# Four layers of cross-attention on one core: the joints between stages reordered, and a launch that waits for fewer constants

## The chip, the cores and the metric

One core of one Trainium2 chip runs the whole program in one launch. The metric is the device time of the execution in microseconds (us), lower is better. TensorE (PE) multiplies, VectorE (DVE) and ScalarE (ACT) work element by element, GpSimd (POOL) helps with copies and sums, and SyncE (SP) issues most transfers.

## The reference, cut to what matters

Four layers follow one another on `x` (4 batches of 256 tokens, width 256) with a context of 1601 rows of width 128. What is computed:

```
L0: qn = layernorm(x); q = qn @ Wq / 8;  k, v = ctx @ Wkv         (16 heads of 64)
    x += tanh(gate) * (softmax(q k^T, masked) v) @ Wo
    x += tanh(gate2) * gelu(layernorm(x) @ W1) @ W2
L1: m = ctx_rows @ W_mem; c = softmax(x m^T / 16) m
    x = rmsnorm(x + sigmoid([x, c] @ W_gate + b) * c) * w
L2: mixed = where(expert, rms(x) @ v_qkv, rms(x) @ l_qkv), rotary, causal self-attention
    x += where(expert, ctx @ v_dense, ctx @ l_dense)
    x += cross-attention(rms(x), ctx; 16 heads of 8) @ cdense
    x += where(expert, silu-MLP with v weights, silu-MLP with l weights)
L3: as L1, with its own weights
```

## The kernel before, in words

The program is written engine by engine: each engine has one list of instructions, in the order in which the Python code issues them, and the engines meet only at semaphores (`Signal` objects; `at(turn, n)` is the value to wait for). No scheduler moves anything. All four batches are unrolled one after another (`body(b, ...)`); the stages of a batch form one chain, and only at its end is the next batch's preparation mixed in.

**The launch.** SP issues the first batch's inputs, then the constants through `const()` (L392 to L395), which all count on one semaphore `const_in`. `const_r` (37 matrices of 128x128, 2.3 MB) lands in `const_r_raw`, placed over the tiles `k_hi_lo0` and `k_hi_rows0`; DVE casts it to `const_r` in `const_cast` (L1470). `const_trig` makes a one-hot matrix of the positions, PE multiplies it with the trigonometric tables (`x<-pos_onehot,const_trig`), and `const_tables` (L1488) copies the result to `cos_t` and `sin_t`. POOL's `prologue` (L511) fills the mask rows of the keys and queries of both buffer sets (`fill_keys`, `fill_queries`). Then come the first projections (`prep_q`, `prep_k`), the first value tiles (`first_values`, seven of them), eight partial maxima (`first_max`, reduced by DVE as `max_parts`) and the first pair of heads.

**Pairs.** The sixteen heads of L0 run as eight pairs (`pair(p)`). Within a pair PE makes 13 score tiles (`st`), ACT takes the exponent (`probs`), POOL adds the tiles up (`prob_sums`, the softmax denominators), PE multiplies with the values (`pv`). The projections of the next pair, the value tiles of the next duo (`v_tile`, written to the bank MI) and the maxima of the next pair are spread between them. `sums(i)` (on PE) multiplies `prob_sums` with ones, DVE takes the reciprocal (`recip_sum`) and scales `attn_t` (`normalise`, which then signals `norm`).

**The joints** are the places where one stage ends and the next starts:

- *Output projection*: after pair 7, `sums` for pair 7, then `x<-w_o,attn_t` for pairs 0 to 6 and last for pair 7; DVE adds to `x_b`, computes mean and variance, POOL raises to the power -1/2 (`rstd_work`), DVE writes `x_normed`, PE transposes it. Ahead of three transposes twelve matmuls (`st<-const_r`, the table `WARM`) run whose result nobody reads. POOL clears `v_cross` (L567) right after its power.
- *Cross-attention of L2*: `cross_queries(0)`, `cross_queries(1)`, then 31 maxima before the first scores; at its end `ctx_heads_t` is divided by its sums (`over_sums`, groups 0 to 2 and then group 3) and multiplied with `w_cd`.
- *Down projection of the MLP*: six `hid` steps on DVE, then `pv<-w_down,...`, for each half of the tokens first six tiles of `h_v`, then six of `h_l`; between the halves PE transposes the next batch's `x_normed`.
- *Pair 0 of each batch*: its value tiles stand behind the score steps k0 = 2, 4, 6, 8, and the first of them waits for DVE's `q_lo_shift` of the next pair.

Of the kernel before, what the change touches and what calls it, by code (L numbers as in the profile page):

```python
# [15 lines left out]
F32 = mybir.dt.float32  # L16
F32R = mybir.dt.float32r
I32 = mybir.dt.int32
# [5 lines left out]
P = 128  # L24
# [12 lines left out]
VS = 4  # L37
# [8 lines left out]
CONSTS = 6  # L46
# [93 lines left out]
def program(nc, io):  # L140

    with ExitStack() as ctx:
# [72 lines left out]
        tids = place("type_ids", [P, NT], I32, [a[0]])  # L215
        side(0, "v", [P, KT, 2 * P], F32)
# [9 lines left out]
        craw_const = place("const_r_raw", [P, N_R, P], F32, [base])  # L226
        posi = place("positions_int", [P, NT], I32, [base + 20480])
        posf = place("positions", [P, NT], F32, [base + 21504])
        onehot = place("pos_onehot", [P, 2, NT], F32, [base + 22528])
        ctrig = place("const_trig", [P, N_C - N_CR, P], F32, [base + 24576])  # L230
# [76 lines left out]
        krows_ready = sig("krows_ready")  # L307
# [36 lines left out]
        cc_read, cc_sum, cc_ready, cd_mm = sig("cc_read", primed=True), sig("cc_sum", 2), sig("cc_ready"), sig("cd_mm")  # L344
# [45 lines left out]
        def _(sp):  # L390
# [87 lines left out]
        def _(pool):  # L478
# [33 lines left out]
            def prologue(b, first):  # L512
# [14 lines left out]
                fill_queries(0)  # L527
                fill_queries(1).then_inc(krows_ready.handle, 1)
                queries(b * PAIRS, 0)
                keys(b * PAIRS, 0, 0)  # L530
                keys(b * PAIRS, 0, 1)

            prologue(0, True)

            def body(b, more):
# [29 lines left out]
                pool.wait_ge(wo_mm.handle, wo_mm.at(b))  # L565
# [33 lines left out]
        def _(act):  # L599
# [33 lines left out]

            act.wait_ge(const_in.handle, CONSTS * 16)
            act.activation(tgate[:], gates[:], ACT.Tanh).then_inc(const_r.handle, 1)
            context(0)
            queries(0, 0)
            act.wait_ge(const_t.handle, const_t.at(0))
            keys(0, 0, 0)
            keys(0, 0, 1)  # L640
# [4 lines left out]
            def body(b, more):  # L645
                def pair(p):
# [12 lines left out]
                    for k0 in range(0, KT, 2):  # L659
# [7 lines left out]
                        if v_tile(p, k0):  # L667
                            if p == 0 and k0 == 2:
# [169 lines left out]
        def _(pe):  # L838
# [18 lines left out]
            def prep_q(i, s, b=None):  # L857

                pe.wait_ge(w_split.handle, w_split.at(i))
# [1151 lines left out]
```

## Time and profile before

| | |
|---|---|
| median of 3 runs | 2308.95 us (2303.93 to 2312.57) |
| the profiled execution | 2304.52 us, of which the span of the trace is 2302.7 us |
| PE busy | 2004.1 us (87%) |
| DVE / ACT / POOL busy | 1298.0 / 923.0 / 766.9 us |
| mean granted TensorE clock | 0.921 |

The profile is of one execution. A busy share says how long an engine had an instruction in flight; the chain of waits says which engine each stretch of the run hung on. The granted clock is 1.00 for 2.4 GHz and 0.50 for 1.2 GHz. A matmul of float32 operands can stand as two records in the trace (16 matmuls of the output projection are 32 records).

### The profile page before, as it was taken

How to read it: one execution, taken by the hardware profiler on the slowest of the kernel's cores; microseconds unless marked ns; L12 is line 12 of the kernel's file. 1: busy time of each engine (PE TensorE's matmuls, PEld its weight loads, DVE VectorE, ACT ScalarE, POOL GpSimd, SP SyncE). 2: the span in 40 equal slices, each digit the busy share in tenths (PEclk: the TensorE clock that was granted, in tenths of full speed). 3: DMA queues.
4: the chain of work that ended last, by engine and by line, in shares of the span. 5: the costliest groups of instructions: out<-in, count | busy, mean ns of one | idle time of the engine just before them, and what ended most of it. 6: DMA issues, size and time to landing. Idle time of an engine off the chain costs nothing.

```text
span 2302.7 us, 30843 instructions
## 1 busy us (share of the span) xinstructions
PE 2004.1 (87%) x11940; PEld 1485.0 (64%) x11940; DVE 1298.0 (56%) x2045; ACT 923.0 (40%) x1718; POOL 766.9 (33%) x676
## 2 busy tenths in 40 slices
PE   3999888898899978899889988889888998888986
PEld 2676667556677657655676766765577765775655
DVE  5666335664676623675576753367457664346733
ACT  1455232371355413257045541326415553231731
POOL 3678410000378731000237881100025886100000
PEclk9999999799899999879999998988999999887998
DMA  4000200201000020100100001020010001102000
GB/s 177 9 11 5 112 1 1 83 1 43 29 12 8 12 104 1 42 41 1 48 26 14 8 37 76 1 83 1 23 36 20 10 8 69 44 1 82 1 1 5
DMA packets 18145, 74.16 MB, mean 32 GB/s; under 512 B 2896, under 2 KB 10320, under 8 KB 14544
## 3 DMA queue, kind: packets, MB, share of 16 engines
q1 hardware_dynamic: 17424, 69.56, 8.2%
q10 hardware_dynamic: 576, 2.62, 0.3%
q8 instruction: 96, 1.57, 0.3%
q14 instruction: 49, 0.40, 0.1%
HBM read 71.13 MB, written 1.05 MB: 31 GB/s over the span
## 4 chain that ended last, share of the span: by engine, by line
PE 68%; DVE 17%; ACT 7%; issue 5%; POOL 2%; DMA 1%; SPq 0%; ACTq 0%; POOLq 0%; DVEq 0%
PE x L841 27%; PE pv L841 18%; PE st L841 15%; PE mi L841 6%; DVE k_hi_lo L1459 3%; ACT k_hi_lo L612 2%; DVE max_parts L1540 2%; POOL prob_sums L555 1%; ACT probs L657 1%; DVE q_lo_shift L1549 1%; DVE prob_sums L1847 1%; PE x L965 1%; DVE x_normed L1640 1%; DVE w_pair_lo L1459 1%; ACT ck_stack L745 1%
## 5 line engine op out<-in xcount | busy, mean ns | idle before, releaser
L555 POOL TENSOR_TENSOR prob_sums<-prob_sums,probs 128x512 f32<-128x512 f32 x352 | 453.6, 1289 | 65.0 <-ACT probs L657 19.0
L657 ACT ACTIVATE probs<-st 128x512 f32<-128x512 f32 x416 | 228.5, 596 | 294.4 <-PE st L841 290.8
L1540 DVE TENSOR_REDUCE max_parts<-x 128x1 f32<-128x832 f32 x256 | 250.7, 1020 | 128.6 <-PE x L841 127.4
L539 POOL TENSOR_TENSOR rstd_work<-rstd_work 128x2 f32<-128x2 f32 x24 | 16.7, 695 | 796.4 <-DVE rstd_work L1456 796.4
L1876 DVE TENSOR_REDUCE max_cross<-x 128x1 f32<-128x512 f32 x384 | 238.8, 684 | 72.0 <-PE x L841 70.5
L841 PE MATMUL st<-q_hi_hi,k_hi_lo 128*128 128x256 f32 x832 | 231.2, 309 | 17.6 <-DVE q_lo_shift L1549 17.6
L841 PE MATMUL pv<-probs,v 128*64 128x256 f32 x1664 | 231.6, 397 | 3.7 <-DVE recip_sum L1664 3.7
L841 PEld LDWEIGHTS st<-q_hi_hi,k_hi_lo 128*128 128x128 f32 x832 | 159.9, 192 | 95.5 <-issue 86.2
L841 PE MATMUL st<-q_lo_shift,k_hi_rows 128*128 128x256 f32 x832 | 210.8, 285 | 0.0
L841 PE MATMUL x<-ck_stack,cq_blocks 128*128 128x512 f32 (+1 forms) x512 | 196.4, 458 | 0.1
L841 PEld LDWEIGHTS st<-q_lo_shift,k_hi_rows 128*128 128x128 f32 x832 | 160.7, 193 | 0.1
L1459 DVE TENSOR_TENSOR k_hi_lo<-x,k_hi_lo 64x832 fp32r<-64x832 f32 x128 | 131.0, 1023 | 40.6 <-ACT k_hi_lo L612 39.3
L841 PEld LDWEIGHTS pv<-probs,v 128*64 128x64 f32 x1664 | 101.1, 137 | 81.5 <-issue 27.1
L841 PE MATMUL x<-k_hi_rows,q_hi 128*128 128x416 f32 x512 | 128.9, 361 | 20.3 <-DVE k_hi_lo L1459 17.6
L841 PEld LDWEIGHTS x<-ck_stack,cq_blocks 128*128 128x128 f32 x512 | 107.6, 226 | 43.8 <-DVE max_cross L1876 32.2
L841 PE MATMUL st<-cq_blocks,ck_stack 128*128 128x512 f32 x280 | 121.6, 443 | 10.6 <-ACT cq_blocks L801 6.5
L1664 DVE RECIPROCAL recip_sum<-pv 128x256 f32<-128x256 f32 x32 | 56.2, 1757 | 108.8 <-PE pv L841 108.8
L612 ACT ACTIVATE k_hi_lo<-x 64x832 fp32r<-64x832 f32 x128 | 110.0, 859 | 17.6 <-PE x L841 15.9
L493 POOL TENSOR_SCALAR k_hi_rows<-k_hi_lo 64x1664 fp32r<-64x1664 f32 x64 | 101.0, 1579 | 38.6 <-ACT k_hi_lo L612 35.7
L841 PEld LDWEIGHTS x<-k_hi_rows,q_hi 128*128 128x128 f32 x512 | 85.3, 190 | 32.9 <-issue 28.9
L819 ACT ACTIVATE probs<-st 128x512 f32<-128x512 f32 x140 | 80.3, 604 | 28.4 <-PE st L841 27.9
L841 PEld LDWEIGHTS st<-cq_blocks,ck_stack 128*128 128x128 f32 x280 | 53.7, 194 | 56.5 <-ACT probs_cross L819 17.1
(291 smaller groups left out, 4158.0 us busy)
## 6 DMA issues: line engine op xcount, KB each, us to landing
w_gate_up<-in_wgu SPq DMA_DIRECT2D x4, 3072.0 KB, 10.1
w_ff<-in_w SPq DMA_DIRECT2D x8, 1024.0 KB, 5.7
w_qk<-in_wqk SPq DMA_DIRECT2D x4, 2048.0 KB, 9.0
w_pair<-in_w SPq DMA_DIRECT2D x32, 192.0 KB, 2.3
w_down<-in_wdn SPq DMA_DIRECT2D x4, 1536.0 KB, 13.4
w_dense<-in_wd SPq DMA_DIRECT2D x4, 1024.0 KB, 12.2
mask_ints<-in_mask SPq DMA_DIRECT2D x4, 832.0 KB, 4.3
ctx_t_raw<-in_ctxT SPq DMA_DIRECT2D x4, 832.0 KB, 5.3
```

Source lines behind the costliest of these rows:

```text
L493: pool.tensor_scalar(t["kh1"][0:64, :, c], r32(t["kst"][0:64, :, c]), 1.0, 0.0, ALU.mult, ALU.add)\
L555: pool.tensor_tensor(acc[:, 0], acc[:, 0], prob[:, kt % 4], ALU.add).then_inc(add_pool.handle, 1)
L612: act.activation(par[s]["kst"][0:64, h, j * HALF:(j + 1) * HALF].rearrange("p (c n) -> p c n", c=2), X[j][64 * h:64 * h + 64, :].rearrange ...
L657: act.activation(prob[:, kt % 4], ST[kt % 2][:], ACT.Exp, scale=HD0 ** -0.5).then_inc(p_exp.handle, 1)
L745: act.activation(ks2[gr][:, j * HALF:j * HALF + n], X[j][:, 0:n], ACT.Identity, bias=ck[:, K_OH_CROSS:K_OH_CROSS + 1])\
L819: act.activation(slot(n), st_bank(n), ACT.Exp, scale=float(HC2) ** -0.5).then_inc(pc_exp.handle, 1)
L841: return pe.matmul(out, lhsT, rhs, start=start, stop=stop, skip_group_check=True)
L965: last = pe.transpose(X[0][:, o:o + P], src[:, t, ch * P:(ch + 1) * P], ident)
L1459: return dve.tensor_tensor(out, x, y, op)
L1540: dve.tensor_reduce(mxs[:, qt, h, half:half + 1], X[n % 2][:].rearrange("p (c n) -> p c n", c=2)[:, :, 0:QUART], AX.XY, ALU.max).then_inc( ...
L1664: dve.reciprocal(rec[:], PV[:, NT:2 * NT]).then_inc(recip.handle, 1)
L1876: t = dve.tensor_reduce(mxc[:, qt, h, c:c + 1], bank, AX.X, ALU.max)
```

## The change

What it does, by joint:

1. **Launch.** `const_r` comes in two pieces, into the tile `probs` and into a place behind `k_hi_rows1`; the positions come first. DVE's `const_cast` and `const_trig` move behind the first splits, PE's `pos_onehot` matmuls behind the first two value tiles and into the bank PV, the other value tiles between the maxima. POOL no longer waits for the constants: it fills buffer set 0, does the first pair's copies, and fills set 1 after them. A new semaphore `side_rows` tells PE that set 1 is filled. ACT's `keys` no longer wait for constants.
2. **Last sums.** `sums` of pair 7 stands behind the first seven `w_o` matmuls.
3. **Cross fill.** POOL's clearing of `v_cross` waits until DVE has written `x_normed`.
4. **Pair 0.** The value tiles move from k0 = 2, 4, 6, 8 to 4, 6, 8, 10.
5. **Cross queries.** `cross_queries(1)` stands behind the first four maxima.
6. **Dense (`w_cd`) in parts.** Groups 0 to 2 after the first division, group 3 after the second; each half of the tokens gets its own bank.
7. **Down in parts.** The tile index is the outer loop; PE starts after the fifth `hid` and waits for the sixth ahead of tile 5.

```diff
@@ launch @@
-            const(craw_const[:], io["const_r"])
+            const(posi[:], io["pos"].partition_broadcast(P))
             const(ctrig[:], io["const_f"][:, N_CR:N_C])
             const(wck[:], io["wckv"])
+            const(prob[:].rearrange("p k (c n) -> p (k c) n", n=P), io["const_r"][:, 0:16])
+            const(craw_const[:], io["const_r"][:, 16:N_R])
             const(gates[:], io["gates"].partition_broadcast(P))
             const(rows[:], io["rows"].partition_broadcast(P))
-            const(posi[:], io["pos"].partition_broadcast(P))
...
                 if first:
-                    pool.wait_ge(const_t.handle, const_t.at(0))
-                    pool.wait_ge(x0t_read.handle, x0t_read.at(0))
                     fill_keys(0)
-                    fill_keys(1)
+                    fill_queries(0).then_inc(krows_ready.handle, 1)
...
                 queries(b * PAIRS, 0)
                 keys(b * PAIRS, 0, 0)
                 keys(b * PAIRS, 0, 1)
+                if first:
+                    fill_keys(1)
+                    fill_queries(1).then_inc(side_rows.handle, 1)
+                    pool.wait_ge(side_rows.handle, side_rows.at(0))
...
             for n in range(8):
                 first_max(0, n)
+                if n < VT - 2:
+                    first_values(0, n + 2)
@@ cross fill @@
                 rsqrt(1)
-                pool.wait_ge(wo_mm.handle, wo_mm.at(b))
+                pool.wait_ge(x_in.handle, x_in.at(b, 1))
@@ last sums @@
-                sums(i0 + PAIRS - 1)
...
                     for t in range(TT):
                         for p in ((PAIRS - 1,) if last else range(PAIRS - 1)):
                             m = mm(X[0][:, t * 512:t * 512 + D], attn[:, p, t * P:(t + 1) * P], wo[:, p], p == 0, p == PAIRS - 1)
+                        if not last and t == 0:
+                            sums(i0 + PAIRS - 1)
@@ pair 0 @@
+            if p == 0:
+                return (1, k0 // 2 - 2) if 4 <= k0 < 4 + 2 * VS else None
@@ cross queries @@
                 cross_queries(0)
-                cross_queries(1)
                 for g in range(CPARTS + LEAD):
+                    if g == 4:
+                        cross_queries(1)
                     cross_max(g)
@@ dense (w_cd) in parts @@
-                pe.wait_ge(cc_ready.handle, cc_ready.at(b))
-                for t in range(TT):
-                    for k in range(4):
-                        m = mm(X[0][:, t * D:(t + 1) * D], cx[:, k, t * P:(t + 1) * P], wcd[:, k], k == 0, k == 3)
+                for last in range(2):
+                    pe.wait_ge(cc_ready.handle, cc_ready.at(b, last + 1))
+                    for t in range(TT):
+                        for k in ((3,) if last else range(3)):
+                            m = mm(X[0][:, t * 512:t * 512 + D], cx[:, k, t * P:(t + 1) * P], wcd[:, k], k == 0, k == 3)
@@ down in parts @@
-                pe.wait_ge(hid.handle, hid.at(b * 6 + 5))
+                pe.wait_ge(hid.handle, hid.at(b * 6 + 4))
                 for t in range(TT):
                     n = 0
-                    for e2, x in enumerate((hv, hl)):
-                        for k in range(6):
+                    for k in range(6):
+                        if t == 0 and k == 5:
+                            pe.wait_ge(hid.handle, hid.at(b * 6 + 5))
+                        for e2, x in enumerate((hv, hl)):
```

PE at the output projection (`x<-w_o,attn_t` are its matmuls, `pv<-prob_sums,const_f` is `sums`), before and with the change:

```order
L841 MATMUL pv<-probs,v_1_88 64x256 x6
L841 MATMUL pv<-prob_sums,const_f 64x256 x2
L841 MATMUL x<-w_o,attn_t 128x256 x16
L841 MATMUL st<-const_r 128x512 x12
L965 MATMUL x<-const_f,x_normed 128x128 x4
```

```order
L846 MATMUL pv<-probs,v_1_88 64x256 x6
L846 MATMUL x<-w_o,attn_t 128x256 x7
L846 MATMUL pv<-prob_sums,const_f 64x256 x2
L846 MATMUL x<-w_o,attn_t 128x256 x9
L846 MATMUL st<-const_r 128x512 x12
```

Seven of the sixteen projection matmuls now stand ahead of `sums`, and so ahead of its wait for POOL.

DVE in the launch, from the variance on (`const_r` is the cast of the constants, `pos_onehot` the positions), before:

```order
L1456 TENSOR_SCALAR rstd_work<-mean_var 128x2
L1473 CAST const_r<-const_r_raw 128x4736
L1578 TENSOR_SCALAR x_normed<-x_in,mean_var,rstd_work 128x256 x2
L1477 CAST positions<-positions_int 128x256
L1478 TENSOR_SCALAR expert_mask<-positions 128x256
L1459 TENSOR_TENSOR positions<-positions,expert_mask 128x256
L1456 TENSOR_SCALAR positions<-positions 128x256
L1456 TENSOR_SCALAR pos_onehot<-positions,const_cols 128x256 x2
```

and with the change:

```order
L1470 TENSOR_SCALAR rstd_work<-mean_var 128x2
L1591 TENSOR_SCALAR x_normed<-x_in,mean_var,rstd_work 128x256 x2
L1470 TENSOR_SCALAR xn_t<-st,lnq_scaled 128x256 x2
L1600 CAST xn_t_hi<-xn_t 128x512
L1473 TENSOR_TENSOR xn_t_lo<-xn_t,xn_t_hi 128x512
L1520 CAST w_pair_hi_106<-w_pair 128x384
L1473 TENSOR_TENSOR w_pair_lo_108<-w_pair,w_pair_hi_106 128x384
L1473 TENSOR_TENSOR ctx_t_lo<-ctx_t_raw,ctx_t_hi 128x832 x2
L1531 CAST w_duo_hi<-w_duo 128x256
L1473 TENSOR_TENSOR w_duo_lo<-w_duo,w_duo_hi 128x256
L1487 CAST const_r<-probs 128x2048
L1488 CAST const_r<-const_r_raw 128x2688
```

The cast, and its wait for the constants, now stands behind nine other steps of DVE.

## Rows read from the trace of the kernel before

**Rows 1.** The page: span, busy time, and the chain that ended last.
```profile
span 2302.7 us, 30843 instructions
PE 2004.1 (87%) x11940; PEld 1485.0 (64%) x11940; DVE 1298.0 (56%) x2045; ACT 923.0 (40%) x1718; POOL 766.9 (33%) x676
PE 68%; DVE 17%; ACT 7%; issue 5%; POOL 2%; DMA 1%; SPq 0%; ACTq 0%; POOLq 0%; DVEq 0%
```

**Rows 2.** Launch, in order of time: start us, us, engine, operation, idle before it.
```profile
20.20 0.69 POOL L515 TENSOR_TENSOR rstd_work<-rstd_work 128x2 f32<-128x2 f32 x1 [19.76 <-DVE rstd_work L1456]
26.23 2.63 DVE L1473 CAST const_r<-const_r_raw 128x4736 fp32r<-128x4736 f32 x1 [6.11 <-DMA positions_int<-in_pos]
35.06 0.42 DVE L1491 COPY cos_t<-x 128x256 f32<-128x256 f32 x1 [0.56 <-PE x L841]
36.09 8.94 POOL L501 TENSOR_SCALAR k_hi_rows<-mask_row,const_cols 64x1664 fp32r<-64x1664 f32 x4 [15.20 <-DVE sin_t L1492]
47.58 4.15 DVE L1459 TENSOR_TENSOR k_hi_lo<-x,k_hi_lo 64x832 fp32r<-64x832 f32 x4
53.75 7.54 DVE L1540 TENSOR_REDUCE max_parts<-x 128x1 f32<-128x832 f32 x8 [2.02 <-PE x L841]
63.03 0.55 PE L841 MATMUL st<-q_hi_hi,k_hi_lo 128*128 128x256 f32 x1 [0.97 <-DVE q_lo_shift L1549]
```

**Rows 3.** By tile, over the whole run: shortest/median/longest ns of one, first and last start.
```profile
L1640 DVE TENSOR_SCALAR x_normed<-x_b,mean_var,rstd_work x8: 632/1923/3215, 271.1 to 1957.1; 128x256 f32<-128x256 f32 x8
L1638 DVE TENSOR_SCALAR x_normed<-x_b,rstd_work x16: 346/351/355, 335.5 to 2221.5; 128x256 f32<-128x256 f32 x16
L1516 DVE CAST w_duo_hi<-w_duo x16: 285/530/1676, 39.9 to 1848.8; 128x256 fp32r<-128x256 f32 x16
```

**Rows 4.** PE at the output projection of batch 0, in order of time.
```profile
258.72 0.65 PE L841 MATMUL pv<-prob_sums,const_f 128*64 128x256 f32 x4 [3.41 <-POOL prob_sums L555]
259.31 8.86 PE L841 MATMUL x<-w_o,attn_t 128*128 128x256 f32 x32
274.88 1.11 PE L965 MATMUL x<-const_f,x_normed 128*128 128x128 f32 x4 [3.95 <-DVE x_normed L1640]
277.08 8.74 PE L841 MATMUL x<-h_t,w_ff 128*128 128x256 f32 x32 [1.09 <-DVE h_t L1456]
285.66 7.07 PE L841 MATMUL pv<-w_ff,gelu_t 128*128 128x256 f32 x32
```

**Rows 5.** DVE and POOL there.
```profile
261.21 0.43 DVE L1459 TENSOR_TENSOR attn_t<-attn_t,recip_sum 128x256 f32<-128x256 f32 x1
271.08 3.60 POOL L567 MEMSET v_cross<- 128x3536 f32 x2
```

**Rows 6.** By stretch, batch 0: us, PE busy (records), granted clock, DMA share, GB/s.
```profile
261.00:263.00 2.00, 2.00 (x6) 0.50 0.00 0
286.00:293.00 7.00, 6.73 (x32) 1.00 0.01 2
530.00:532.00 2.00, 2.00 (x6) 0.50 0.00 0
541.00:544.00 3.00, 2.88 (x7) 0.50 0.00 0
```

**Rows 7.** End of the cross-attention of batch 0.
```profile
528.59 5.41 PE L841 MATMUL x<-w_cd,ctx_heads_t 128*128 128x256 f32 x16 [2.31 <-DVE ctx_heads_t L1459]
```

**Rows 8.** The other joints of batches 0 and 1, PE.
```profile
566.61 2.86 PE L841 MATMUL pv<-w_down,h_v 128*128 128x256 f32 x12 [1.85 <-DVE h_l L1459]
421.35 0.58 PE L841 MATMUL mi<-cq_hi,const_r 128*128 128x256 f32 x1 [2.05 <-ACT cq_blocks L794]
633.70 0.35 PE L841 MATMUL mi<-w_duo_hi,ctx_t_hi 128*128 128x256 f32 x1 [2.85 <-DVE q_lo_shift L1459]
```

**Rows 9.** DVE beside the down projection of batch 0.
```profile
568.57 2.01 DVE L1578 TENSOR_SCALAR x_normed<-x_in,mean_var,rstd_work 128x256 f32<-128x256 f32 x2 [0.87 <-POOL rstd_work L515]
577.71 0.69 DVE L1459 TENSOR_TENSOR x_a<-pv,x_b 128x512 f32<-128x512 f32 x1 [0.21 <-PE pv L841]
```

More of the change, by code:

```diff
@@ L45 @@
 EPS = (1e-5, 1e-5, 1e-6, 1e-6, 1e-6, 1e-6, 1e-6)
-CONSTS = 6
+CONSTS = 7
 LNQ_G, LNQ_B, LNF_G, LNF_B, W_IN, W_CROSS, W_POST = range(0, 14, 2)
@@ L215, in program @@
         tids = place("type_ids", [P, NT], I32, [a[0]])
+        craw_const = place("const_r_raw", [P, N_R - 16, P], F32, [a[0] + 1024])
         side(0, "v", [P, KT, 2 * P], F32)
@@ L225, in program @@
         attn = place("attn_t", [P, PAIRS, NT], F32, a)
[L226 to L230, printed above, removed]
+        posi = place("positions_int", [P, NT], I32, [base + 27648])
+        posf = place("positions", [P, NT], F32, [base + 28672])
+        onehot = place("pos_onehot", [P, 2, NT], F32, [base + 29696])
+        ctrig = place("const_trig", [P, N_C - N_CR, P], F32, [base + 31744])
         wck = place("w_ckv", [P, 2, P], F32, [base + 26624])
@@ L526, in prologue @@
                     fill_keys(0)
-                fill_queries(0)
-                fill_queries(1).then_inc(krows_ready.handle, 1)
+                    fill_queries(0)
+                    fill_queries(1).then_inc(krows_ready.handle, 1)
                 queries(b * PAIRS, 0)
@@ L632, in first_values @@
                 values(b, 0, c, ST[c % 2])
+            context(0)
+            queries(0, 0)
+            keys(0, 0, 0)
+            keys(0, 0, 1)
             act.wait_ge(const_in.handle, CONSTS * 16)
             act.activation(tgate[:], gates[:], ACT.Tanh).then_inc(const_r.handle, 1)
[L636 to L640, printed above, removed]
+            act.wait_ge(const_t.handle, const_t.at(0, 1))
             act.wait_ge(types_read.handle, types_read.at(0))
@@ L667, in pair @@
                         if v_tile(p, k0):
-                            if p == 0 and k0 == 2:
+                            if p == 0 and k0 == 4:
                                 act.wait_ge(done.handle, done.at(b, 0))
@@ L859, in prep_q @@
                 pe.wait_ge(w_split.handle, w_split.at(i))
+                if i == 1:
+                    pe.wait_ge(side_rows.handle, side_rows.at(0))
                 if b is not None:
@@ L935, in _ @@
             x0_transposed(0)
+            for n in range(4):
+                mm(PV[:], ident, cc[:].rearrange("p k n -> p (k n)"))
+            prep_q(0, 0, 0)
+            prep_k(0, 0, 0, 0)
+            prep_k(0, 0, 1, 0)
+            for c in range(2):
+                first_values(0, c)
             pe.wait_ge(const_in.handle, CONSTS * 16)
@@ L939, in _ @@
                 for ch in range(2):
-                    last = mm(X[1][:, k * NT:(k + 1) * NT], ctrig[:, tab - N_CR + ch], onehot[:, ch], ch == 0, ch == 1)
+                    last = mm(PV[:, k * NT:(k + 1) * NT], ctrig[:, tab - N_CR + ch], onehot[:, ch], ch == 0, ch == 1)
             last.then_inc(const_r.handle, 1)
-            for n in range(4):
-                mm(PV[:], ident, cc[:].rearrange("p k n -> p (k n)"))
-            prep_q(0, 0, 0)
-            pe.wait_ge(const_t.handle, const_t.at(0))
-            prep_k(0, 0, 0, 0)
-            prep_k(0, 0, 1, 0)
-            for c in range(VT):
-                first_values(0, c)
             for n in range(8):
                 first_max(0, n)
+                if n < VT - 2:
+                    first_values(0, n + 2)
             first_shifts(0)
+            pe.wait_ge(const_t.handle, const_t.at(0))
             def body(b, more):
@@ L1031, in pair @@
                     if p < PAIRS - 1:
-                        if v_tile(p, 2):
-                            d, c = v_tile(p, 2)
-                            pe.wait_ge(v_read.handle, v_read.at(b * DUOS + d, VS if c == 0 else VT))
+                        if v_tile(p, 4):
+                            d, c = v_tile(p, 4)
+                            pe.wait_ge(v_read.handle, v_read.at(b * DUOS + d, VS if c < VS else VT))
                         pe.wait_ge(q_lo.handle, q_lo.at(i + 1))
@@ L1472, in const_cast @@
                 dve.wait_ge(const_in.handle, CONSTS * 16)
-                dve.tensor_copy(cr[:], craw_const[:]).then_inc(const_t.handle, 1)
+                dve.tensor_copy(cr[:, 0:16].rearrange("p k n -> p (k n)"), prob[:].rearrange("p k n -> p (k n)"))
+                dve.tensor_copy(cr[:, 16:N_R], craw_const[:]).then_inc(const_t.handle, 1)
             def const_trig():
@@ L1609, in _ @@
             x0_normed(0)
-            const_trig()
             x0_scaled(0)
-            const_tables()
             split(0, 0)
@@ L1616, in _ @@
             split_v(0, 0)
+            const_cast()
+            const_trig()
             split(0, 1)
@@ L1625, in _ @@
             neg_max(0)
+            const_tables()
             shifts(0, 0)
```

16 lines of the change are left out of this document (7 added, 9 removed).

## Prediction

> **What bounds the kernel now.** I read the page first: PE is busy 87% of the span of 2302.7 us, and the chain that ended last runs on PE for 68% and on DVE for 17% [rows 1]. So the run is one chain of stages, mostly on PE, and a gap in PE at a joint is time of the run, not time hidden behind something else. The second view is PE's waits at the joints in order of time: PE stands 3.41 us for POOL's last addition, 3.95 us for `x_normed` [rows 4], 2.31 us for a division [rows 7], 1.85 us for the last `hid`, 2.05 us for `cross_queries`, 2.85 us for `q_lo_shift` [rows 8]. All of these but the last recur once per batch. The third view is the launch: DVE has its variance at 20.9 us and then stands until 26.23 us for the last constant, and the first scores start at 63.03 us [rows 2]. The fourth is the granted clock by stretch. Behind the long gaps it is at 0.50, the 1.2 GHz level, although PE is busy then; 261 to 263 us follows the 3.41 us gap [rows 6]. So a gap costs twice: its own length, and slow matmuls behind it. The 32 records of the output projection take 8.86 us and the 32 of the first feed-forward product 8.74, against 7.07 for 32 equal ones that run at the full clock [rows 4]: 1.8 and 1.7 us from the clock. One record at full clock is 7.07/32 = 0.22 us.
>
> The sum below is made against the profiled execution, 2304.5 us. That is 4.4 us under the median of the three runs.
>
> **Part by part.**
>
> *Last sums, 4 batches.* PE is free 3.41 us before 258.72, at 255.3 [rows 4]. With the change 14 records (7 matmuls) run at once, 14 x 0.22 = 3.1 us, to 258.4; POOL's sum is there at 258.7 as before; `sums` 0.65 us, to 259.4; 14 records, to 262.5; the last pair's scaled `attn_t` is ready at 261.64, as DVE starts its reciprocal when it did [rows 5]; four records, to 263.4. Before, the projection ended at 268.17. Gain 4.8 us per batch, 19 in all. If the slow clock behind the gap stayed, it would be 3.0 us, the gap that is filled (12 in all): the lower bound.
>
> *Cross fill, 4 batches.* DVE's `x_normed` at this joint takes 632 to 3215 ns a piece, against 351 for the same shape elsewhere [rows 3], and POOL's clearing starts in the same instant, 271.08 us, and lasts 3.60 us [rows 5]. DVE waits for the end of POOL's instruction. With the change POOL starts after it, beside a stretch in which DVE reads PSUM only and then idles; the cleared tile is first written to by `cross_v`, two stages later. The two pieces last 3.77 us in batch 0 and would take 0.7: 3.1 us. The gap of PE ahead of its transposes falls from 3.95 to about 0.9, so some of the 1.7 us of slow feed-forward goes too. I take half, as another gap of 1.09 us follows: 4.0 per batch, 16 in all, between 12 and 19. The Trainium skill (SBUF — State Buffer, section on the two separate sides) describes this: VectorE in a two-port mode and GpSimd share a port pair as an exclusive lock for a whole instruction. The 3215 ns beside the clearing agree.
>
> *Dense (`w_cd`) in parts, 4 batches.* Groups 0 to 2 were divided long before; PE has waited 2.31 us, since 526.3, when it goes on at 528.59 for group 3 [rows 7]. Now 12 of the 16 records fill this wait, 2.6 us, to 528.9; then four, 0.9 us: 529.8. Before, the end was at 528.59 + 5.41 = 534.0. Gain 4.2 us, 17 in all, of which 1.9 per batch is the slow clock (16 records in 5.41 against 3.5 us). Without the clock, 2.3 per batch (9).
>
> *Down in parts.* PE starts 1.85 us earlier [rows 8]; ten of the twelve products per half do not need the sixth `hid`. In batches 0 to 2 the transposes between the halves need the next batch's `x_normed`, ready at 570.6 [rows 9]; the first half (24 records, 5.2 us) now ends at 570.0 instead of 571.8, so PE waits 0.6 us there, and DVE, whose list of small steps left only 0.21 us of slack before `x_a` [rows 9], moves ahead with the transposes. Gain 1.2 us three times and 1.85 in the last batch: 5.
>
> *Cross queries, 4 batches.* The first maximum no longer stands behind the second query block: two records, 0.6 us. The 2.05 us of waiting stay, since they are ACT's time for the first block [rows 8]. DVE's reductions set the pace afterwards, so 0.6 x 4 = 2.4.
>
> *Pair 0.* In batches 1 to 3 PE waited 2.85 us for `q_lo_shift` ahead of the first value tile [rows 8]. The wait moves behind two more score tiles and two `pv` tiles, but the next thing, a maximum, needs DVE's four `k_hi_lo` pieces (4.15 us in the launch [rows 2]), which end where they did. So one wait takes the place of the other; I keep 0.8 us three times: 2.4, between 0 and 6. In batch 0 nothing.
>
> *Launch, once.* DVE sets the pace, and its work up to the last `k_hi_lo` is the same list in another order. Before, it ran from the cast at 26.23 to 47.58 + 4.15 = 51.73 us with one wait of 0.56 (for the tables) [rows 2]: 24.9 us of work, of which 0.8 (the copies of the tables) now stands behind the maxima. With the change it starts at the end of POOL's power, 20.20 + 0.69 = 20.9, and has one new wait, for PE's transposes of `x_normed`, 1.2 us (the length that the transposes have elsewhere [rows 4]): 20.9 + 24.9 - 0.8 + 1.2 = 46.2. The eight maxima follow without the 2.02 us wait (the value tiles ran ahead of them on PE and now run between them): 7.5, to 53.7. From the last maximum to the first scores it took 63.03 - 61.29 = 1.7, and 0.3 of the copies stick out: 55.8 instead of 63.03. The constants are there at 26.2 to 27, before DVE comes to them. Gain 7.
>
> What could eat it: POOL's fills now start at 20.9, beside `x_normed` and the splits; before, they met DVE from 36.09 on. `w_duo_hi` took 1676 ns there and 285 at its shortest [rows 3], so a collision costs DVE about 1.4 us. As many collisions as before are in the 24.9 us already. Three more, and a slow PE behind its wait for the positions, which must pass before the maxima, would leave 1 us; none at all would give 12. Where DVE reads PSUM it isn't held: four `k_hi_lo` take 4.15 us beside POOL's fills [rows 2]. I take 7.
>
> By the skill's rule of the lock (same page and section; it also covers two-input operations against a GpSimd operation that reads SBUF) every step of DVE in 21 to 42 us that reads SBUF twice could lose a fill's whole length. By the trace it is about 1.4 us for a step that meets a fill, and that is what the sum contains.
>
> *Sum*: 19 + 16 + 17 + 5 + 2.4 + 2.4 + 7 = 69 us. 2304.5 - 69 = 2235.5. As the runs' median lies 4.4 us above the profiled one, I say 2237.
>
> **The rivals.**
>
> *The slow clock stays.* The gaps shrink but PE's clock falls behind them as before, since small waits remain at each joint (0.3 to 1.1 us). For it: behind the joint into the MLP, whose gaps no part of the change touches, the clock is at 0.50 as well [rows 6]. Against it: it is full in the second feed-forward product, which has no gap ahead of it [rows 6]. Then the joints give 12 + 12 + 9 + 5 + 2.4 + 2.4 and the launch 7: 50 us, 2255. Chance 0.22.
>
> *The launch gives nothing*, because POOL's fills and DVE's splits now collide from the start: 69 - 6 = 63 us, 2242, or 2246 with a lost microsecond at each batch's first pair. It differs from the forecast mostly in place. Chance 0.15.
>
> *Better than the sum*: the clock effects in full and the launch with few collisions, 69 + 3 + 5 + 4 = 81 us, 2224. Chance 0.12.
>
> *Slower.* PE would be held to a lower clock because it idles less. The chain has 68% of the span on PE, 1566 us [rows 1]; each per cent of clock lost there costs 15.7 us, so a mean granted clock of 0.921 that fell by more than 4.4%, below 0.88, would eat all 69 us. At a fall of 5% the time is 2235.5 + 78 = 2314. Against it: the clock reads 1.00 where PE is densest and 0.50 behind gaps [rows 6]. The Trainium skill (TensorE: Matmul & The Clock Gate, Part 1) says the same: the half rate is the resting state and activity lifts it; its power limit concerns several busy cores. Chance 0.02, and 0.02 for a result within 0.5%. That the change doesn't do what it says is excluded for the orders of instructions, which are written out.
>
> **How the numbers follow.** Forecast 0.47 (2230 to 2243), slow clock 0.22, launch 0.15, better 0.12, same 0.02, slower 0.02. The likeliest time is 2237. The range reaches to the better case and to the slow clock with 4 us of run-to-run difference: 2218 to 2258. 0.5% of this kernel is 11.5 us, about what a measurement can tell from no change; every case but the last two is faster by more.
>
> **What would show it.** In the changed profile: no wait of PE for `prob_sums` over 0.5 us and `w_o` done about 8 us after the last `pv`; `x_normed` at this joint under 0.4 us a piece; `w_cd` without its 2.31 us wait; the granted clock at 1.00 behind these joints; first scores at 56 us; mean clock above 0.93. The slow clock rival is right if `w_o` and the first feed-forward product still need over 8.5 us. The forecast is wrong if a stage of equal work (pairs 1 to 7, the cross-attention between its joints) becomes longer than before.

## The result and the profile after

| | before | with the change |
|---|---|---|
| median of 4 runs on one chip | 2307.18 us (2303.93 to 2312.57) | 2244.31 us (2240.4 to 2249.35) |
| ratio, 95% interval | | 0.9729 [0.9711, 0.9748] |
| profiled execution / span | 2304.52 / 2302.7 us | 2243.16 / 2241.4 us |
| mean granted TensorE clock | 0.921 | 0.935 |

The change takes 61.3 us off the span; 69 were predicted. The median lies 7 us above the predicted 2237 and inside the range of 2218 to 2258. The page of the changed kernel, as [rows 1] of before:

```profile
span 2241.4 us, 30844 instructions
PE 1978.9 (88%) x11940; PEld 1467.1 (65%) x11940; DVE 1287.9 (57%) x2046; ACT 923.3 (41%) x1718; POOL 765.9 (34%) x676
PE 68%; DVE 19%; ACT 7%; issue 4%; POOL 2%; ACTq 0%; POOLq 0%; DVEq 0%
```

PE does the same 11940 matmuls in 25 us less, which is mostly the clock; the other 36 us were idle time. The chain is still 68% PE. The line numbers have moved: the matmul helper is L846 now (L841 before), the transposes L974 (L965).

**The joints one by one.** I cut both traces into stages at the same instructions (the first score, DVE's write of `x_b`, the first `w_ff` matmul and so on) and compared the lengths. Each number is the difference of two starts; minus is faster:

| stage | batch 0 | 1 | 2 | 3 | gain | predicted |
|---|---|---|---|---|---|---|
| start to first scores | -2.96 | | | | 3.0 | 7 |
| first scores to the first `attn_t` (pair 0) | +0.44 | +0.99 | +0.90 | +0.94 | -3.3 | 2.4 |
| last `attn_t` to `x_b` (last sums) | -4.69 | -4.63 | -4.78 | -4.67 | 18.8 | 19 |
| `x_b` to `x<-h_t,w_ff` (cross fill) | -3.50 | -3.03 | -3.04 | -3.49 | 13.1 | 16 with the next row |
| feed-forward | +0.12 | +0.26 | -1.41 | +0.17 | 0.9 | |
| up to the first cross maximum (cross queries) | -0.48 | -0.89 | -0.43 | -2.03 | 3.8 | 2.4 |
| cross-attention and `w_cd` (dense) | -4.14 | -4.88 | -4.19 | -3.17 | 16.4 | 17 |
| MLP to `x_a` (down) | -2.26 | -1.03 | -2.27 | -1.21 | 6.8 | 5 with the next row |
| `x_a` to the next first scores | +0.09 | +0.91 | +2.08 | | -3.1 | |

These rows give 56.4 us. The other 5 lie in stages that the change doesn't touch; 3.75 of them in one place, the self-attention of batch 3, where the granted clock before was 0.55 (2054 to 2063 us) and is now 1.00. So the orders of matmuls did most of what the sum says. Two rows are off, the launch and pair 0, and a smaller one is the feed-forward behind the cross fill. The last row, `x_a` to the next first scores, is not the change's alone: it is 46.5, 44.5 and 44.5 us before, and in kernels that leave the down projection as it was it also lies anywhere between 44.4 and 46.6.

**The output projection**, PE and then DVE and POOL, in order of time, as [rows 4, 5]:

```profile
252.19 3.29 PE L846 MATMUL x<-w_o,attn_t 128*128 128x256 f32 x14
255.69 0.65 PE L846 MATMUL pv<-prob_sums,const_f 128*64 128x256 f32 x4 [0.20 <-POOL prob_sums L560]
256.27 4.15 PE L846 MATMUL x<-w_o,attn_t 128*128 128x256 f32 x18
260.07 3.11 PE L846 MATMUL st<-const_r 128*128 128x512 f32 x12
264.10 0.66 PE L974 MATMUL x<-const_f,x_normed 128*128 128x128 f32 x4 [0.92 <-DVE x_normed L1654]
265.84 8.86 PE L846 MATMUL x<-h_t,w_ff 128*128 128x256 f32 x32 [1.09 <-DVE h_t L1470]
```

```profile
263.31 0.73 DVE L1654 TENSOR_SCALAR x_normed<-x_b,mean_var,rstd_work 128x256 f32<-128x256 f32 x2 [0.82 <-POOL rstd_work L544]
264.17 3.57 POOL L572 MEMSET v_cross<- 128x3536 f32 x2 [0.89 <-DVE x_normed L1654]
```

The wait for `prob_sums` is 0.20 us instead of 3.41. All 32 projection records (14 + 18) run near 0.23 us each: the slow stretch behind the old gap is gone. The two pieces of `x_normed` take 0.73 us together, with the clearing behind them, and PE waits 0.92 us instead of 3.95. But the first feed-forward product still takes 8.86 us against 7.07 at the full clock. That is the part of the cross fill that didn't come.

**The two other joints**, as [rows 7, 8]:

```profile
514.96 3.62 PE L846 MATMUL x<-w_cd,ctx_heads_t 128*128 128x256 f32 x16
...
554.14 0.66 PE L859 MATMUL st<-const_f,x_normed 128*128 128x128 f32 x4 [0.69 <-DVE x_normed L1591]
```

`w_cd` runs in one piece without a wait, 3.62 us instead of 2.31 of waiting and 5.41 of work. In the down projection the predicted new wait of 0.6 us, for the next batch's `x_normed`, is there with 0.69.

**Pair 0 of batch 1.** Where before had one wait of 2.85 us [rows 8], there are three:

```profile
616.10 0.36 PE L846 MATMUL mi<-w_duo_hi,ctx_t_hi 128*128 128x256 f32 x1 [0.69 <-DVE q_lo_shift L1473]
...
618.19 0.61 PE L846 MATMUL x<-k_hi_rows,q_hi 128*128 128x416 f32 x2 [1.15 <-DVE k_hi_lo L1473]
620.27 0.62 PE L846 MATMUL x<-k_hi_rows,q_hi 128*128 128x416 f32 x2 [1.47 <-DVE k_hi_lo L1473]
```

0.69 + 1.15 + 1.47 = 3.31 us. The maxima now meet DVE's four `k_hi_lo` pieces with too little in front of them. Before, the value tiles behind them covered those pieces.

**The launch.** DVE, then POOL, then PE, as [rows 2]:

```profile
34.07 1.62 DVE L1493 TENSOR_SCALAR expert_mask<-positions 128x256 f32<-128x256 f32 x1
35.72 1.74 DVE L1473 TENSOR_TENSOR positions<-positions,expert_mask 128x256 f32<-128x256 f32 x1
37.50 1.64 DVE L1470 TENSOR_SCALAR positions<-positions 128x256 f32<-128x256 f32 x1
39.17 1.89 DVE L1470 TENSOR_SCALAR pos_onehot<-positions,const_cols 128x256 f32<-128x256 f32 x2
...
45.73 4.15 DVE L1473 TENSOR_TENSOR k_hi_lo<-x,k_hi_lo 64x832 fp32r<-64x832 f32 x4
```

```profile
33.97 3.23 POOL L496 TENSOR_SCALAR k_hi_rows<-k_hi_lo 64x1664 fp32r<-64x1664 f32 x2
37.29 3.36 POOL L504 TENSOR_SCALAR k_hi_rows<-mask_row,const_cols 64x1664 fp32r<-64x1664 f32 x2
```

```profile
41.21 3.47 PE L846 MATMUL pv<-pos_onehot,const_trig 128*128 128x256 f32 x8 [7.56 <-DVE pos_onehot L1470]
...
60.07 0.55 PE L846 MATMUL st<-q_hi_hi,k_hi_lo 128*128 128x256 f32 x1 [0.97 <-DVE q_lo_shift L1564]
```

Three small steps of DVE on the positions take 1.6 to 1.7 us each, and the two of `pos_onehot` 1.89 together. 1.6 to 1.7 us is the length of one of POOL's instructions beside them (3.23/2 and 3.36/2). The first scores start at 60.07 us, not at 56.

### The profile page after: what moved, and what is told of

Its sections match the earlier page's. It is cut to its first block, busy times and chain, and to the rows that moved or that the text cites. A ratio compares the mean times of both kernels' runs of the same rounds, so it can differ in the third digit from the quotient of the medians.

```text
span 2241.4 us, 30844 instructions
## 1 busy us (share of the span) xinstructions
PE 1978.9 (88%) x11940; PEld 1467.1 (65%) x11940; DVE 1287.9 (57%) x2046; ACT 923.3 (41%) x1718; POOL 765.9 (34%) x676
## 4 chain that ended last, share of the span: by engine, by line
PE 68%; DVE 19%; ACT 7%; issue 4%; POOL 2%; ACTq 0%; POOLq 0%; DVEq 0%
PE x L846 26%; PE pv L846 18%; PE st L846 16%; PE mi L846 6%; DVE k_hi_lo L1473 3%; ACT k_hi_lo L617 2%; DVE max_parts L1555 1%; DVE max_cross L1890 1%; ACT probs L662 1%; POOL prob_sums L560 1%; DVE q_lo_shift L1564 1%; DVE prob_sums L1861 1%; PE x L974 1%; ACT ck_stack L750 1%; DVE recip_sum L1768 1%
## 5 line engine op out<-in xcount | busy, mean ns | idle before, releaser
L846 PE MATMUL st<-q_hi_hi,k_hi_lo 128*128 128x256 f32 x832 | 230.9, 309 | 17.8 <-DVE q_lo_shift L1564 17.8
L846 PE MATMUL pv<-probs,v 128*64 128x256 f32 x1664 | 231.2, 397 | 3.7 <-DVE recip_sum L1678 3.7
L846 PEld LDWEIGHTS st<-q_hi_hi,k_hi_lo 128*128 128x128 f32 x832 | 159.7, 192 | 95.6 <-issue 84.8
L846 PE MATMUL st<-q_lo_shift,k_hi_rows 128*128 128x256 f32 x832 | 210.8, 285 | 0.0
L846 PE MATMUL x<-ck_stack,cq_blocks 128*128 128x512 f32 (+1 forms) x512 | 193.4, 441 | 10.6 <-ACT cq_blocks L799 8.2
L846 PEld LDWEIGHTS st<-q_lo_shift,k_hi_rows 128*128 128x128 f32 x832 | 160.5, 193 | 0.1
L846 PE MATMUL x<-k_hi_rows,q_hi 128*128 128x416 f32 x512 | 131.9, 366 | 31.1 <-DVE k_hi_lo L1473 30.0
L846 PEld LDWEIGHTS pv<-probs,v 128*64 128x64 f32 x1664 | 101.0, 137 | 82.3 <-issue 29.4
L846 PEld LDWEIGHTS x<-ck_stack,cq_blocks 128*128 128x128 f32 x512 | 104.2, 218 | 53.2 <-DVE max_cross L1890 31.6
L846 PE MATMUL st<-cq_blocks,ck_stack 128*128 128x512 f32 x280 | 122.7, 448 | 10.6 <-ACT cq_blocks L806 6.5
L846 PEld LDWEIGHTS x<-k_hi_rows,q_hi 128*128 128x128 f32 x512 | 86.1, 193 | 44.0 <-issue 42.2
L846 PEld LDWEIGHTS st<-cq_blocks,ck_stack 128*128 128x128 f32 x280 | 54.2, 196 | 56.8 <-ACT probs_cross L824 17.1
```

Source lines behind the costliest of these rows:

```text
L846: return pe.matmul(out, lhsT, rhs, start=start, stop=stop, skip_group_check=True)
```

## Experiments

The kernel before ran beside each group of experiments, with medians of 2309.5 to 2309.8 us (the first eight kernels) and 2306.4 us (the last four). So ratios are what may be compared across groups. The changed kernel itself ran only beside the before of 2307.18 us. Down in parts and cross queries have no run of their own.

### Pair 0 put back

```diff
-            if p == 0:
-                return (1, k0 // 2 - 2) if 4 <= k0 < 4 + 2 * VS else None
...
```

> The changed kernel with the value tiles of pair 0 back at k0 = 2 to 8. Theory: moving them cost 0.9 to 1.0 us in each of batches 1 to 3 and 0.4 in batch 0, because PE now stands before two maxima for DVE's k_hi_lo (0.69 + 1.15 + 1.47 us) instead of 2.85 us before one value tile. Then pair 0 takes 25.6 us again instead of 26.5 in batches 1 to 3, and the run 2240 us, 3.3 us less than the changed kernel. Rival: the 0.9 us are drift of the TensorE clock and not of the order; then pair 0 stays at 26.5 us and the run at 2244.

2243.29 us, ratio 0.9712 [0.9691, 0.9733]. The run doesn't differ measurably from the changed kernel. The stage does: from the first scores to the first `attn_t` it is 1.54, 2.27, 2.21 and 0.98 us shorter than in the changed kernel. One long wait is back,

```profile
615.50 0.35 PE L844 MATMUL mi<-w_duo_hi,ctx_t_hi 128*128 128x256 f32 x1 [2.85 <-DVE q_lo_shift L1471]
```

and it costs less than the three short ones. From the first `attn_t` to the last, batches 0, 1 and 3 took 1.4 to 1.5 us longer in this trace, with the same instructions. That takes back 4 of the 7 us; the first scores come 1.2 us later, and other untouched stages lose the rest. What those 1.4 us are comes up again below. A comparison over all traces settles more. Four of the kernels here have pair 0's value tiles in their new place, and ten in the old one. In batches 1 to 3 the stage takes 30.3 to 30.4 us in all of the four, and in the ten 26.6 to 29.4, mostly 29.4. So the new place costs 0.9 us or more per batch.

### Sums, dense, fill and launch each alone

Four kernels put one part of the change into the kernel before. Last sums alone (`sums(i0 + PAIRS - 1)` moved behind the first seven `w_o` matmuls):

> The kernel before with only the last sums behind the first seven output-projection matmuls. Theory: the stretch from the last attn_t to x_b falls from 12.8 to 8.15 us in every batch, as in the changed kernel, 4.7 us each and 19 in all: 2290. The clearing of v_cross still holds x_normed (1.9 us a piece), and the clock behind it is slow as before. Rival: without the other edits the gap only moves behind the projection, and the run gains 12 us or less, 2297.

2290.6 us, 0.9919 [0.9897, 0.9942], 19 us faster. The stage to `x_b` is 4.6 to 4.7 us shorter in each batch.

Dense alone (`w_cd` in two parts, two banks):

> The kernel before with only the product with w_cd in two parts. Theory: w_cd takes 3.6 us and starts without the 2.31 us wait, so the stretch from the first cross maximum to x_b is 4.1 us shorter in every batch, 16.5 in all: 2292. Rival: the 1.9 us of slow clock in it belong to the phase of the clock and not to the wait; then 2.3 us per batch, 2300.

2290.37 us, 0.992 [0.9893, 0.9946], 19 us faster; the stage is 4.2, 4.2, 6.1 and 4.0 us shorter. Both parts are worth what the sum gave them, and don't depend on the rest.

Cross fill alone:

```diff
-                pool.wait_ge(wo_mm.handle, wo_mm.at(b))
+                pool.wait_ge(x_in.handle, x_in.at(b, 1))
```

> The kernel before with only POOL's clearing of v_cross held until x_normed is written. Theory (a lock between the two engines): x_normed falls from 1.9 us a piece to 0.36 in all batches, the stretch from x_b to the first feed-forward product from 8.4 to 8.9 us to 5.4, and the slow clock behind it stays: 3.0 to 3.5 us per batch, 2296 for the run. Rival of the prediction: the shorter gap brings back half of the slow clock too, 4.0 us per batch, 2293. If the clearing were not the cause, 2308.

2284.28 us, 0.9888 [0.9861, 0.9914]: 25 us, more than any theory. The profiled executions differ by 21 us, of which 19 lie in the two stages of this edit; the rest lies in untouched stages. The joint gives 3.0 to 3.5 us, as in the changed kernel, and here the feed-forward gives 1.4 to 1.6 more in every batch, since its clock is full:

```profile
259.42 1.07 PE L841 MATMUL pv<-prob_sums,const_f 128*64 128x256 f32 x4 [3.41 <-POOL prob_sums L555]
260.42 8.39 PE L841 MATMUL x<-w_o,attn_t 128*128 128x256 f32 x32
...
272.49 0.66 PE L965 MATMUL x<-const_f,x_normed 128*128 128x128 f32 x4 [0.92 <-DVE x_normed L1640]
274.24 7.17 PE L841 MATMUL x<-h_t,w_ff 128*128 128x256 f32 x32 [1.09 <-DVE h_t L1456]
```

PE has the same waits of 0.92 and 1.09 us as in the changed kernel, and yet one product takes 7.17 us here and 8.86 there. The projection ahead of it is slow here (8.39) and full there. That doesn't decide it either: with pair 0 put back, batch 0 has the same two waits (0.93 and 1.09 us), a projection at the full clock and a feed-forward product of 7.17 us.

Launch alone:

> The kernel before with the launch part of the change alone: the constants' loads and first steps are not waited for ahead of the first keys. Theory (the copies and fills on POOL stretch DVE's small position steps, so most of the early start is given back): the first scores start at 60 to 61 us instead of 63, the run gains 2 to 3 us, near 2306.5. Rival (the early start is worth its full 7 us when the other parts are absent): first scores at 56, run near 2302.

2303.7 us (10 runs against 13 of before), 0.9986 [0.9972, 1.0]: 3 us, at the edge of what these runs can tell from nothing. The first scores start at 60.77 us, as the theory says; the early start is not worth 7 us even when nothing else is changed. Its trace has a third form of the same joint, with before's order of instructions:

```profile
255.84 0.65 PE L844 MATMUL pv<-prob_sums,const_f 128*64 128x256 f32 x4 [3.38 <-POOL prob_sums L558]
256.42 7.17 PE L844 MATMUL x<-w_o,attn_t 128*128 128x256 f32 x32
...
270.30 0.66 PE L972 MATMUL x<-const_f,x_normed 128*128 128x128 f32 x4 [3.96 <-DVE x_normed L1647]
272.05 10.19 PE L844 MATMUL x<-h_t,w_ff 128*128 128x256 f32 x32 [1.09 <-DVE h_t L1463]
```

The gap of 3.38 us was followed by a projection at the full clock, and the slow stretch fell into the feed-forward: 10.19 us instead of 8.74. So a gap doesn't always bring a slow stretch right behind it; both products together take 17.4 us here and 17.6 before.

The four gains are 19 + 19 + 25 + 3 = 66 us, and the whole change gives 63 on its medians (2307.2 against 2244.3). With what the stages of down (3.7), cross queries (3.8) and pair 0 (-3.3) measure in the changed kernel, the parts add up to some 8 us more than the whole. 5 of these are the clock that the fill wins in the feed-forward alone (5.9 us) and not in the changed kernel's trace (0.9). The other 3 are within the spread of the medians.

### POOL held at the launch

```diff
+                if first:
+                    pool.wait_ge(types_read.handle, types_read.at(0))
                 queries(b * PAIRS, 0)
...
                 if first:
+                    pool.wait_ge(types_read.handle, types_read.at(0))
                     fill_keys(1)
```

POOL's copies of the first keys and queries, and its fills of buffer set 1, wait until DVE is through with its small steps.

> The changed kernel, in whose launch POOL waits for DVE's last SBUF step (the token types) before it copies the first pair's queries and keys and fills buffer set 1. Theory: the launch gained 3 us instead of 7 because DVE's small steps on the positions met POOL's copies and fills, 1.3 to 1.7 us each instead of 0.3 to 0.4. Then these steps take 0.3 to 0.5 us each, DVE ends its list some 6 us earlier, POOL's copies are then late for the maxima by about 2 us, and the first scores stand at 55 to 57 us instead of 60.07. Rival: DVE's steps are long for another reason (transfers at the launch); then they stay at 1.6 us and the first scores come at 61 us or later.

2238.2 us, 0.9694 [0.9668, 0.9721]. The first scores start at 53.08 us, 7.0 earlier than in the changed kernel:

```profile
33.11 0.29 DVE L1496 TENSOR_SCALAR expert_mask<-positions 128x256 f32<-128x256 f32 x1
33.44 0.42 DVE L1476 TENSOR_TENSOR positions<-positions,expert_mask 128x256 f32<-128x256 f32 x1
33.90 0.29 DVE L1473 TENSOR_SCALAR positions<-positions 128x256 f32<-128x256 f32 x1
34.23 0.61 DVE L1473 TENSOR_SCALAR pos_onehot<-positions,const_cols 128x256 f32<-128x256 f32 x2
...
38.68 4.15 DVE L1476 TENSOR_TENSOR k_hi_lo<-x,k_hi_lo 64x832 fp32r<-64x832 f32 x4
```

The same steps take 0.29, 0.42, 0.29 and 0.61 us. `k_hi_lo` starts at 38.68 instead of 45.73: the whole gain stands in this list. This settles the launch. The scores come even 2 us earlier than the expected 55 to 57, since POOL's held copies weren't late: DVE goes from `k_hi_lo` to its maxima with waits of under 0.2 us. The Trainium skill (SBUF — State Buffer, section on the two separate sides) says that GpSimd and a VectorE operation in a two-port mode (or one with two SBUF inputs, against a GpSimd operation that reads SBUF) share a port pair, which whichever starts first keeps for its whole instruction. The trace agrees, as a step of 0.29 us becomes 1.62 beside an instruction of 1.6. The four `k_hi_lo`, which read one operand from PSUM, take 4.15 us in both kernels, beside POOL's copies here and without them in the changed kernel.

With only the fills held, and the copies as in the change:

> The changed kernel with only the fills of the second set of operands held on POOL until the position codes are read; the copies of the first keys run as they do now. It splits what the held version gained at the launch (first scores 60.1 to 53.1 us). Theory (copies and fills each stretch the DVE steps that they lie beside): the first scores start near 57 us. Rival (the fills alone do it): 53 to 54. Rival (the copies alone): 60.

First scores at 57.46 us, as the theory expected. `k_hi_lo` starts at 42.05 us, so of the 7.05 us the fills cost 3.7 and the copies 3.4. The run's ratio is 0.9738 [0.972, 0.9756], no gain over the changed kernel's 0.9729, though its first scores come 2.6 us earlier: at two or three microseconds a start is read from the trace and not from the run.

### Four unread matmuls behind the transposes

```diff
+TAIL = {1: 4}
...
                     last.then_inc(xt_mm.handle, 1)
+                    for n in range(TAIL.get(k, 0)):
+                        mm(ST[0][:], cr[:, R_ID], cr[:, R_SELF:R_SELF + 4].rearrange("p k n -> p (k n)"))
```

They stand in the 1.09 us in which PE waits for `h_t`, and add nothing that is read.

> The changed kernel with four more matmuls that nobody reads right behind the transposes of the output projection's joint, while PE waits 1.09 us for h_t. Theory: the first feed-forward product still takes 8.86 us (7.07 at the full clock) because PE's clock falls behind the three small waits of the joint (0.92, 0.75 and 1.09 us); with the last of them filled it takes 7.1 to 7.5 us and the run is 5 to 7 us shorter than the changed kernel, 2238. Rival: the clock falls for the waits ahead of the transposes or for none of them; then the product stays at 8.4 to 8.9 us and the run at 2244.

2240.73 us, 0.9706 [0.9684, 0.9727]; the interval overlaps that of the changed kernel, so the run alone shows nothing. The stage from the start of `w_ff` to `x_a` takes 14.12 us in every batch, and took 15.81 in three of four. One trace would not be enough: of the five kernels that have the cross fill and no unread matmuls here, the others have 14.12 us in three batches (pair 0 put back, both with POOL held) or in all four (fill alone), 14 of 20 in all. But in the four kernels with these unread matmuls and the fill it is 14.12 in all 16 batches. So they make the full clock sure where it was a matter of chance.

```profile
262.89 0.66 PE L975 MATMUL x<-const_f,x_normed 128*128 128x128 f32 x4 [0.93 <-DVE x_normed L1657]
263.30 1.17 PE L847 MATMUL st<-const_r 128*128 128x512 f32 x4
264.63 7.17 PE L847 MATMUL x<-h_t,w_ff 128*128 128x256 f32 x32 [0.16 <-DVE h_t L1473]
```

The granted clock in this stretch, changed kernel first (start and end, length, busy time of PE, PEld, DVE, ACT and POOL, clock, DMA share, GB/s):

```profile
267.00:270.00 3.00, 3.00 (x9) 2.38 (x8) 0.00 (x0) 0.00 (x0) 1.96 (x6) 0.58 0.96 404
```

```profile
266.00:270.00 4.00, 4.00 (x20) 3.51 (x20) 0.00 (x0) 1.02 (x1) 1.74 (x5) 1.00 0.96 401
```

0.58 against 1.00, at the same DMA load (404 and 401 GB/s), which excludes the transfers as the cause. The lower of the two is a mixture of the levels 1.2 and 2.4 GHz.

### The three remedies together, and more unread matmuls

Pair 0 as before, POOL held, four unread matmuls:

> The changed kernel with pair 0 as before, POOL's copies held in the launch, and the four matmuls behind the output projection's transposes. Theory: the three gains add: first scores at 53 us (7.0 us), pair 0 in 24.3 to 25.6 us instead of 26.5, the first feed-forward product at the full clock. From 2244: 7 + 4 + 5 us, 2229. Rival: slow stretches of the clock of 1.5 us each come back elsewhere, as behind pair 0 in the run that undid it, and half of it is lost: 2236.

2233.63 us, 0.9682 [0.9654, 0.9709]. The feed-forward is at 14.1 us in all batches; the first scores start at 55.21 us, 2.1 later than in the held version. DVE's list ends at the same time in both (42.8 us). Behind it the granted clock is 0.50 from 44 to 48 us here and 0.95 or more there, and DVE stands 0.95 us ahead of two of the maxima: the slow clock again. So 11 us under the changed kernel, not 15.

To this, more unread matmuls (the keys of the two tables are the joints, the values the counts; `WARM` stands ahead of the transposes, `TAIL` behind them): key 1 is the joint into the feed-forward, and more are now added at those into the cross-attention (4) and the MLP (5) of L2.

```diff
-WARM = {1: 12, 4: 12, 5: 12}
-TAIL = {1: 4}
+WARM = {1: 15, 4: 20, 5: 17}
+TAIL = {1: 4, 4: 4, 5: 10}
```

> As the run before it, with more unread matmuls around the other warmed joints: 15, 20 and 17 ahead of the transposes instead of 12, and four (query projection of the cross-attention) and ten (MLP) behind them, all in stretches in which PE waits. Theory: the first six gate and up products run at the full clock, 1.9 us per batch, and the cross-attention's query projection too, 1 us; 2229 - 11 = 2218. Rival: the slow clock falls on later work or the added matmuls delay the transposes; then 2229 or more.

2211.08 us, 0.9573 [0.955, 0.9597]; 23 us for 120 further matmul records that nobody reads, and 7 better than expected. 15 us of them lie in the two stages with the joints that got more. The mean granted clock is 0.955.

Next, the same unread matmuls in the kernel before, and nothing else:

> The kernel before, its order untouched, with unread matmuls alone placed ahead of and behind the joints where PE waits. Theory (part of what a joint costs is the lower clock that follows it): the granted clock rises from 0.92 to about 0.94 and the run falls by 15 to 20 us, to about 2291, with every wait for the last sums and the fill still there. Rival (the joints cost only their waits): no change, within 0.3% of the kernel before, or a few us longer for the added matmuls.

2288.77 us, 0.9923 [0.9908, 0.9938]: 18 us, at an order of real work that is untouched. The clock is 0.937 in place of 0.921. At the joint into the cross-attention of batch 0 (before's rows, then this kernel's):

```profile
413.38 1.11 PE L965 MATMUL x<-const_f,x_normed 128*128 128x128 f32 x4 [2.33 <-DVE x_normed L1638]
415.46 2.07 PE L841 MATMUL mi<-x_t,w_cq 128*128 128x256 f32 x4 [0.97 <-DVE x_t L1794]
```

```profile
411.27 0.66 PE L966 MATMUL x<-const_f,x_normed 128*128 128x128 f32 x4 [0.50 <-DVE x_normed L1641]
411.68 1.17 PE L842 MATMUL st<-const_r 128*128 128x512 f32 x4
412.90 1.13 PE L842 MATMUL mi<-x_t,w_cq 128*128 128x256 f32 x4
```

`x_normed` comes as late as ever, but transposes and queries take 0.66 and 1.13 us instead of 1.11 and 2.07. The stage up to the first cross maximum is 1.7 to 2.2 us shorter per batch, the MLP's 1.7 to 2.65, together 17.7 us and so the whole gain. So part of what a wait costs can be had back without touching the wait.

At last, unread matmuls at the joints that still had none, key 3 being the one into the self-attention (`WARM` 3: 13 and `TAIL` 2: 3, 3: 9, 6: 3, and ten more in each memory layer):

> The best version so far (2211) with more unread matmuls: 13 ahead of the cross joint, 3 to 10 behind the transposes of each joint, 6 ahead of the keys' normed rows. Theory (the remaining stretches at the lower clock, five of 1.6 us per batch, follow waits that no unread matmul covers yet): two of them per batch go, 4 x 3.3 = 13 us, to 2198. Rival (those stretches follow no wait and move about): no change, 2211, or slower by the time of the added matmuls, up to 2216.

2204.34 us, 0.9566 [0.9539, 0.9594], the same as 0.9573: the rival was right. The trace is of the slowest of the four executions (2214.65 us, clock 0.956 against 0.962 to 0.966), so only what recurs in every batch is read from it. The first memory layer gains 0.2 to 1.6 us per batch, and the stage ahead of the self-attention loses 3.06 in each:

```profile
317.54 3.27 PE L848 MATMUL st<-const_r 128*128 128x512 f32 x13 [1.08 <-ACT ck_stack L752]
320.64 0.60 PE L976 MATMUL x<-const_f,x_normed 128*128 128x128 f32 x4
```

The wait for ACT stands ahead of the thirteen, and the transposes behind them: they fill no wait and stand on the path, 3.1 us. An unread matmul is free only where it lies *ahead of* a wait and fits into it.

## Why the prediction was right, and where not

**The bound, and the four joints.** PE's chain with its gaps was the right reading: last sums 18.8 against 19, dense 16.4 against 17, cross queries 3.8 against 2.4, and down with what follows 3.7 against 5. The single-part runs confirm the first two; the other two are read from the one trace. The gain of the first two was waiting and clock, as [rows 6] said: per batch, `w_o` ran 1.4 us faster and `w_cd` 1.8 (3.29 + 4.15 against 8.86, and 3.62 against 5.41), of gains of 4.7 and 4.1.

**The total is in part luck.** The stages that the change touches gave 56.4 us of the 69. The other 5 came from stages that it doesn't touch, 3.75 of them from one slow stretch of the clock that wasn't there this time. The predicted time has a slip as well: 2235.5 us and the 4.4 us to the median make 2240, not 2237.

**Cross fill, 14 against 16.** The 3.1 us of `x_normed` came. The term that was off is "I take half" of the feed-forward's slow clock: it came in one batch of four, 0.9 us of 3.4. By this trace the clock rival was right for this product and wrong for `w_o` and `w_cd`. But the other kernels with this joint got it in three or four batches of four, so a half was no bad guess of a thing that varies from execution to execution. Unread matmuls in the next wait bring it every time.

**The launch, 3 against 7.** The failed step is "As many collisions as before are in the 24.9 us already". DVE's list from `x_normed` to the last `k_hi_lo`, without its wait of 1.27 us for the transposes, took 20.6 us with POOL held and 27.5 in the change; the sum had 24.1. Before, four splits lost 5.2 us beside POOL's fills (`w_duo_hi` took 1.68 instead of 0.28). They got that back. But POOL's work moved beside smaller steps: the small steps that the lines of the launch show lose 5.3 us, `x_normed` 1.3, and several others some 2 in all. That is 3.4 us more than predicted, and the eight maxima took 0.8 more (8.3 against 7.5). The text named this as what could eat the gain, and priced it too low by taking the old number of collisions for a new overlap.

**Pair 0, a loss of 3.3 against a gain of 2.4.** The failed step is "the next thing, a maximum, needs DVE's four `k_hi_lo` pieces", "which end where they did", with the conclusion "So one wait takes the place of the other". The direction was seen and not followed: the maxima come in a row, each behind its piece, with less work in front of them, so one wait became three. The range "between 0 and 6" had left out a loss without a reason that excludes one. The loss is shown by the stage, which is longer in every trace with the new place; the run with pair 0 put back was no faster.

**What would be seen.** The wait for `prob_sums`, `x_normed`, `w_cd` and a mean clock above 0.93 came as named; first scores at 56 us did not. Untouched stages did become up to 2 us longer in places, which the prediction had named as a sign against it; others became shorter by more. No lower clock from a busier PE is to be seen: the mean rose from 0.921 to 0.935.

## What to carry to other kernels

Ahead of a wait for another engine, put matmuls that don't need what is waited for; where none are left, put unread ones ahead of the wait, never behind it, and look at the granted clock of the stage that follows. When work of POOL moves, list which DVE steps it will now lie beside, and count each short SBUF step as long as the POOL instruction that it meets. When a wait is moved, write down the waits of the next several instructions at the new place, not of the next one only.

## What was not expected of the hardware

The slow clock comes in pieces. From `attn_t` of pair 1 to that of pair 7 the instructions are identical in all kernels; in 42 of 56 cases this took 139.9 to 140.1 or 141.4 to 141.6 us, and between 139.4 and 142.9 in the others. The feed-forward behind the cross fill took 14.12 or 15.81. Such pieces of 1.4 to 1.7 us appear behind short waits (0.92 and 1.09 us in the changed kernel), are absent behind the very same waits in other kernels, and once skipped the product behind a wait of 3.38 us. What decides this stays open; the trace shows the granted clock and not why it is granted. Its consequence is practical: a change of 2 or 3 us can be hidden or doubled by where the pieces fall, so such a change is judged by its stage.

The kernel with all of the change except pair 0, POOL held at the launch and unread matmuls at three joints runs at 0.957 of the time before (2211 us), 1.6% below the changed kernel.
